# The first attention with its weights computed a second time, keys on the partitions, instead of being transposed

## The chip, the cores and the metric

The kernel runs on one core of one Trainium2 chip. The metric is the device time of one execution in microseconds (us), as the median of the runs shown. TensorE multiplies matrices, VectorE (DVE in the rows) and ScalarE (ACT) read and write PSUM and SBUF, GpSimd (POOL) works on SBUF only, and SyncE (SP) issues the DMAs.

## The reference, cut to what matters

```python
# B, N, D = 8, 512, 128; all float32
# 1: layer norm with shift and scale from c @ wmod, then causal attention with 16 heads of dimension 8
q = x @ Wq.T ;  k, v = split(x @ Wkv.T)
sim = einsum('bhid,bhjd->bhij', q * 8 ** -0.5, k);  sim = where(causal_mask, -max_float, sim)
m = max(sim, axis=-1);  e = exp(sim - m)
out = einsum('bhij,bhjd->bhid', e, v) / (sum(e, axis=-1) + 1e-8)
x = x + gate * (out @ Wo.T)
# 2: a second modulated norm, then six layers of (local attention with rotary tables, norm, gated feed-forward)
```

The change touches the attention of part 1 alone.

## The kernel before, in words

`adaln_block` runs three blocks one behind the other: `modulated_attention` (the first attention and the norms around it), `local_stack` (the six layers) and `last_residual`. Everything of the first two is kept with the dimensions on the partitions and the tokens along the free axis.

In `modulated_attention` each engine runs its own program, `batch(b)`, for b = -1 to 8, where b = 1 to 6 are turns of a hardware loop. A batch has 16 steps s, one for each head. What a step does for head s and for heads some steps back is written out in each engine's `batch`; `head_of(s, back)` names the head. Semaphores alone tie the engines together, and each engine takes its instructions in the written order. At the edges (`alive`) work of batches that don't exist is left out.

A head of 512 queries is done as four row tiles of 128 queries. Row tile i sees the keys 0 to (i + 1) * 128, so the tiles are 128, 256, 384 and 512 columns wide, 1280 together.

1. Projections. Four heads make a group. For each group, the jobs `q` and `k` (L1101) give a 128-row product whose 128 rows are four copies of the group's 32 dimensions. ScalarE rounds it (`high`, L1161 to L1165) and VectorE subtracts that from the full value in some of the copies (L1294, L1301), so that one product of two rounded operands sums high and low parts. For each head, VectorE writes `qm`, the group's q with the rows of the other three heads set to zero (`pick_head`, L1337).
2. Scores. `score` (L1056) is one matmul of rounded float32 for a row tile, into that tile's own bank; it waits until the exponential of the same tile of the head before is done.
3. VectorE adds the causal mask to the diagonal block (`mask`, L1343) and takes the negated row maximum (`maximum`, L1347).
4. ScalarE takes the exponential with the maximum as bias and the row sum as a second output (L1191, which issues an ACTIVATE and an ACTIVATION_READ_ACCUMULATOR).
5. VectorE takes the reciprocal of the four row sums (`reciprocals`, L1355, L1357), GpSimd multiplies the four row tiles by it (L1426).
6. Three steps behind, TensorE transposes the ten 128x128 blocks of the head (L1069) in two parts, ScalarE copies them out of PSUM (L1201).
7. `round` (L1095): for the four heads of a group, the weights by the values, each head in 32 columns of the array, so that four matmuls run side by side; VectorE copies the result to `aT` (L1314). `wo` (L1110) is the output projection, L1307 the gated residual.

The products other than scores and transposes (`q`, `k`, `v`, `round`, `wo`, the transposes of x, the means and variances of the norms) share one bank, `ps_m`, in the order of a hand-written list `M_JOBS` of (step, part, kind, batch offset, group). Part 0 stands inside the step, part 1 at its end. Each waits until the one before has been taken from the bank.

The norms end with one Newton step for the reciprocal root on VectorE (`finish_norm`, L1264 to L1284). GpSimd also prepares the six layers' weights and tables in the loop turns (`split`, L1408 and L1410; `rotary_tables`, L1399), and SP loads and stores them around `load(b)` and `store(b)`.

Of the kernel before, what the change touches and what calls it, by code (L numbers as in the profile page):

```python
# [7 lines left out]
ALU = mybir.AluOpType  # L8
# [5 lines left out]
P = 128  # L14
# [12 lines left out]

HID = int(DIM * 4 * 2 / 3)
# [6 lines left out]
LN_EPS = 1e-5  # L35

# [11 lines left out]
C_HEAD = C_ROT + TILES * 2 * 2 * DH  # L48
C_LOW = C_HEAD + 4
# [3 lines left out]
C_END = C_ONE + 1  # L53


def shape_constants():
# [23 lines left out]
    c[:, C_ROT:C_HEAD] = tables.reshape(TILES, P, 2 * 2 * DH).transpose(1, 0, 2).reshape(P, -1)  # L80
# [3 lines left out]

    row = np.arange(P)
    c[:, C_HEAD:C_LOW] = row[:, None] % 32 // 8 == np.arange(4)[None, :]
    c[:, C_LOW] = -1.0 * (row // 64 == 1)
    c[:, C_LOW + 1] = -1.0 * (row // 32 % 2 == 1)
# [3 lines left out]
def constant_views(consts):  # L92
# [9 lines left out]
        "head": consts[:, C_HEAD:C_LOW],  # L102
# [4 lines left out]
        "one": consts[:, C_ONE:C_END],  # L107
# [734 lines left out]
AH = 16  # L842
AD = DIM // AH
ATT_EPS = 1e-8

GROUP = 4
GROUPS = AH // GROUP
GP = P // GROUP
SCORE_BANKS = 4

ROW_AT = [i * (i + 1) // 2 * P for i in range(TILES)]
ROWS_END = TILES * (TILES + 1) // 2 * P

KEY_AT = {0: 0, 1: 512, 3: 896, 2: 1024}
PROB_BUFS, PROBT_BUFS = 4, 8

SPLIT_STEPS = (2, 9, 13)
TABLE_STEPS = (0, 4, 6, 11)


def modulated_attention(nc, w, const_sb, mod, xT, x_done, x1_dram, w_split, tables):

    ident, ones_mean, causal, head, low_q, low_k, one = (
        const_sb[k] for k in ("ident", "ones_mean", "causal", "head", "low_q", "low_k", "one"))
# [14 lines left out]
    with ExitStack() as ctx:  # L890
# [6 lines left out]
        def bank(name, n=1):  # L897
# [5 lines left out]
        wmod = sb("wmod", [P, 6 * DIM])  # L903
        wqk = sb("wqk", [P, 2, GROUPS, P])
# [8 lines left out]
        q_full = sb("q_full", [P, N])  # L913
        high = sb("high", [P, N], F32R)
        q4, k4 = sb("q4", [P, 2, N], F32R), sb("k4", [P, 2, N], F32R)
        qm = sb("qm", [P, 2, N], F32R)
        v_pad = sb("v_pad", [P, TILES, AH, GP])
        probs = sb("probs", [P, PROB_BUFS, ROWS_END])
        probT = sb("probT", [P, PROBT_BUFS, ROWS_END])
        nmx = sb("nmx", [P, 2, TILES])  # L920
        den = sb("den", [P, 2, TILES])
        rden = sb("rden", [P, 2, 2, TILES])
        aT = sb("aT", [P, GROUPS, N])
        qk_scale = sb("qk_scale", [P, 2, DEPTH, 2 * DH])
# [4 lines left out]
        ps_score = [bank(f"score{i}") for i in range(SCORE_BANKS)]  # L929
        ps_t = bank("t", 3)  # L930
        ps_m = bank("m")
# [7 lines left out]
        zeroed = sem("zeroed")  # L939
# [5 lines left out]
        rden_own, weights_ready = (  # L945
            sem(k) for k in ("rden_own", "weights_ready"))

        t_ready, t_copied = [sem("t_ready_0"), sem("t_ready_1")], [sem("t_copied_0"), sem("t_copied_1")]

# [593 lines left out]
```

## Time and profile before

| | us |
|---|---|
| median of 3 runs | 4414.89 (4414.82 to 4419.62) |
| the profiled execution | 4412.12, with a span of 4410.3 |
| first attention and its norms | from 0 to 877.6 of the span |
| local stack | from there to about 4390 |

The profile is of one execution. Its page gives the busy time of each engine over the whole span; the views used below are a table of windows, which cuts the span into stages, the waits, the groups of instructions by line and shape, and stretches of the timeline. A row of the timeline merges instructions of one line that run on: its second number runs from the first one's start to the last one's end, and the mark "x4" says how many. The clock column is the share of TensorE's full clock that was granted.

### The profile page before, as it was taken

The numbers are of one execution on the slowest core, as the hardware profiler recorded it, in microseconds if no ns is written. First come the engines' busy times: TensorE is split into PE (matmuls) and PEld (weight loads), VectorE is DVE, ScalarE is ACT, GpSimd is POOL, SyncE is SP. The second block draws the span as 40 slices with busy tenths as digits, with TensorE's granted clock in tenths as the row PEclk, the third lists the DMA queues.
The fourth block names the chain that finished last, engine by engine and source line by source line (L and its number), as shares of the span: only waits on it lengthen the run. The fifth ranks groups of instructions, "written<-read, shape, count | busy, mean of one in ns | idle before, by whom it ended". The sixth has DMA issues, their size and how long they took to land. (4 is left out here: it accounts for less than half of the span.)

```text
span 4410.3 us, 109941 instructions
## 1 busy us (share of the span) xinstructions
PE 3768.9 (85%) x41516; PEld 2856.2 (65%) x41516; DVE 3571.7 (81%) x5298; ACT 2656.4 (60%) x4035; POOL 2895.4 (66%) x2520
## 2 busy tenths in 40 slices
PE   5666666669999899998999989999899999899996
PEld 3444444357777777776777767777677777677774
DVE  6777777678888788887888878888888888888884
ACT  5666666546666566656566656656566656566663
POOL 3555555357777677676767666777677676667672
PEclk9888888889999999999999999999999999999998
DMA  1111111032222322223222232222322222222221
GB/s 38 53 53 53 53 53 45 8 90 64 55 60 56 92 59 62 56 58 91 62 55 62 56 88 65 55 58 54 89 60 67 56 56 78 70 60 63 56 55 58
DMA packets 157205, 267.21 MB, mean 61 GB/s; under 512 B 32062, under 2 KB 51644, under 8 KB 152380
## 3 DMA queue, kind: packets, MB, share of 16 engines
q1 hardware_dynamic: 157116, 266.19, 22.1%
q8 instruction: 36, 0.59, 0.1%
q14 instruction: 53, 0.43, 0.0%
HBM read 44.81 MB, written 26.21 MB: 16 GB/s over the span
## 5 line engine op out<-in xcount | busy, mean ns | idle before, releaser
L789 POOL TENSOR_TENSOR st_qk_rot<-st_qk_rot,st_qk_sq 128x1024 f32<-128x1024 f32 x384 | 920.4, 2397 | 939.6 <-DVE st_qk_sq L686 939.6
L429 PE MATMUL st_ps<-st_wqkv,st_xs 128*128 128x512 f32 x3456 | 956.7, 412 | 66.2 <-DMA st_wqkv<-wqkv_parts 37.7
L537 ACT ACTIVATE st_qk_sq<-st_ps 128x1024 f32<-128x1024 f32 x384 | 393.9, 1026 | 652.6 <-PE st_ps L429 652.0
L429 PEld LDWEIGHTS st_ps<-st_wqkv,st_xs 128*128 128x128 f32 x3456 | 612.4, 190 | 231.4 <-issue 97.8
L809 POOL TENSOR_TENSOR st_qk_rot<-st_qk_rot,st_rn 128x1024 f32<-128x1024 f32 x384 | 722.7, 1903 | 15.0
L1426 POOL TENSOR_TENSOR at_probs<-at_probs,at_rden 128x128 f32<-128x128 f32 (+3 forms) x512 | 361.8, 738 | 389.6 <-DVE at_rden L1357 389.6
L668 DVE TENSOR_REDUCE st_nt<-st_qk_sq 128x16 f32<-128x1024 f32 x384 | 465.7, 1213 | 175.5 <-ACT st_qk_sq L537 175.4
L686 DVE TENSOR_TENSOR st_qk_sq<-st_ps,st_rot 128x512 f32<-128x512 f32 x768 | 490.2, 678 | 0.0
L672 DVE TENSOR_TENSOR st_qk_rot<-st_ps,st_rot 128x1024 f32<-128x1024 f32 x384 | 465.9, 1213 | 8.6 <-PE st_ps L444 8.6
L444 PE MATMUL st_ps<-consts_sb,st_qk_rot 128*128 128x128 f32 x3072 | 403.0, 274 | 27.9 <-DVE st_hid L769 16.5
L437 PEld LDWEIGHTS st_ps<-st_oT,st_wo 128*128 128x128 f32 x3072 | 368.8, 192 | 79.4 <-issue 75.8
L1191 ACT ACTIVATE at_probs<-at_score,at_nmx 128x128 f32<-128x128 f32 (+3 forms) x512 | 269.1, 527 | 249.0 <-DVE at_nmx L1347 244.3
L444 PEld LDWEIGHTS st_ps<-consts_sb,st_qk_rot 128*128 128x128 f32 x3072 | 357.1, 141 | 93.7 <-DVE st_hid L769 36.3
L568 ACT ACTIVATE st_k_bd<-st_ps 64x1024 f32<-64x1024 f32 x384 | 389.4, 1014 | 3.7 <-PE st_ps L444 1.4
L437 PE MATMUL st_ps<-st_oT,st_wo 128*128 128x128 f32 x3072 | 379.2, 277 | 1.4 <-ACT st_probT L598 1.2
L457 PE MATMUL st_ps<-st_k_bd,st_qT 128*32 128x128 f32 x12288 | 376.1, 275 | 1.8 <-ACT st_v_tok L582 1.8
L1056 PE MATMUL at_score<-at_k,at_qm 128*128 128x128 f32 (+3 forms) x512 | 239.9, 510 | 159.8 <-ACT at_probs L1191 117.6
L469 PE MATMUL st_ps<-st_v_bd,st_probT 128*32 128x128 f32 x12288 | 375.2, 274 | 0.0
L837 POOL TENSOR_TENSOR st_s<-st_s,st_mx 128x1024 f32<-128x1024 f32 x192 | 365.8, 1905 | 9.9 <-DVE st_mx L711 9.9
L707 DVE TENSOR_TENSOR st_s<-st_ps,consts_sb 128x1024 f32<-128x1024 f32 x192 | 234.5, 1221 | 146.4 <-PE st_ps L457 146.4
L457 PEld LDWEIGHTS st_ps<-st_k_bd,st_qT 128*32 128x32 f32 x12288 | 324.4, 110 | 34.4 <-ACT st_v_tok L582 26.2
L469 PEld LDWEIGHTS st_ps<-st_v_bd,st_probT 128*32 128x32 f32 x12288 | 323.8, 110 | 23.0
(125 smaller groups left out, 6828.4 us busy)
## 6 DMA issues: line engine op xcount, KB each, us to landing
st_v_bd<-st_v_tok SPq DMA_DIRECT2D x1152, 128.0 KB, 2.3
st_v_bd<-st_v_tok SPq DMA_DIRECT2D x672, 64.0 KB, 2.1
wqkv_parts<-at_w_parts SPq DMA_DIRECT2D x18, 1024.0 KB, 4.5
st_wqkv<-wqkv_parts SPq DMA_DIRECT2D x18, 1024.0 KB, 5.7
at_w_raw<-in_wqkv SPq DMA_DIRECT2D x18, 512.0 KB, 4.1
rotary_tables<-at_rot SPq DMA_DIRECT2D x6, 512.0 KB, 2.8
st_rot<-rotary_tables SPq DMA_DIRECT2D x24, 128.0 KB, 2.4
st_wo<-in_wo SPq DMA_DIRECT2D x6, 512.0 KB, 4.2
```

The costliest lines, as they stand in the source:

```text
L429: last = pe.matmul(out[:, c * 512:(c + 1) * 512], xs[:, x_part, t * P:(t + 1) * P], rhs, start=(n == 0), stop=(n == len(PASSES) - 1))
L437: last = pe.matmul(out[:, 0:P], wo[:, c, :], oT[:, c * P:(c + 1) * P], start=(c == 0), stop=(c == IC - 1))
L444: last = pe.transpose(out[:, c * P:(c + 1) * P], src[:, c * P:(c + 1) * P], ident)
L457: last = pe.matmul(out[g * WIN:(g + 1) * WIN, c * P:(c + 1) * P], qT[:, par, c * P + g * WIN:c * P + (g + 1) * WIN], k_bd[:, c, :, key:key ...
L469: last = pe.matmul(out[g * WIN:(g + 1) * WIN, c * P:(c + 1) * P], probT[:, c * P + g * WIN:c * P + (g + 1) * WIN], v_bd[:, par, g, :, c * ...
L537: act.activation(qk_sq[:, cols_of(a)], slot_of("qk"[a], 0, t), ACT.Square).then_inc(squared[a], 1)
L568: last = act.activation(k_bd[rows, :, a, WIN + t1 * P:WIN + (t1 + 1) * P], src[rows, :, :], ACT.Copy)
L668: dve.tensor_reduce(nt[:, 2 + par, heads], qk_sq[:, cols].rearrange("p (h d) -> p h d", d=DH), AX.X, ALU.add).then_inc(ss_sum, 1)
L672: dve.tensor_tensor(qk_rot[:, cols].rearrange("p (h d) -> p h d", d=DH), slot_of("qk"[a], 0, t).rearrange("p (h d) -> p h d", d=DH), rot[: ...
L686: last = dve.tensor_tensor(dst[:, :, g, :], src[:, :, 1 - g, :], sines.unsqueeze(1).to_broadcast([P, HEADS, DH // 2]), ALU.mult)
L789: pool.tensor_tensor(qk_rot[:, cols], qk_rot[:, cols], qk_sq[:, cols], ALU.add).then_inc(rot_done[a], 1)
L809: pool.tensor_tensor(view, view, rn[:, par, heads_of(a)].unsqueeze(2).to_broadcast([P, HEADS, DH]), ALU.mult).then_inc(normed[a], 1)
```

## The change

- The scores are computed twice. The first time as before, by rows, for the maximum alone. The second time with keys on the partitions and queries on the columns (`scores_by_key`), six steps behind (`LAG`). The second product holds the weights already in the layout in which `round` wants them, so ScalarE's exponential writes `probT` directly, and the transposes, their copies, `probs`, and GpSimd's multiplication go.
- The rows of a group are laid out anew: head c has rows 32c to 32c + 31, 8 of them spare. A score matmul uses the 32 rows of its head alone, so `qm` goes. The negated maximum of each query is put into two of the spare rows of q as a high and a low part, where k has ones: the second product comes out with the maximum subtracted. `max_parts`, `max_rest`, the transposes `mt` and one addition on VectorE per group do that. The low-by-low product is not formed, and the factor 8 ** -0.5 moves into the exponential.
- The causal mask is added on TensorE, as a product of the identity and the mask that accumulates onto the scores, in both products.
- The row sum is a column of ones beside v: it comes out of `round` in row 8 of each head's 32. The jobs `den` (4 matmuls with 4 columns), a reciprocal and a copy on VectorE, `rd` (4 transposes) and a multiplication of `aT` do the division per group, after `round`. ScalarE takes `round` out of the bank.
- Three units a head instead of four row tiles: (512), (384 and 128), (256), each in one bank. The other jobs get two banks in turn, with a new list. The Newton step of the norms goes to GpSimd; `split` and `rotary_tables` stand at other steps, and SP stores x1 after the second split and the tables.

```diff
+    part, of_max = row % 32 // 8, row % 32 < 2
+    c[:, C_LOW] = -1.0 * (part == 3)
+    c[:, C_LOW + 1] = -1.0 * (part == 2) + of_max
+ROW_UNITS = (((3, 0),), ((2, 0), (0, 3 * P)), ((1, 0),))
+KEY_UNITS = ((0,), (1, 3), (2,))
-SPLIT_STEPS = (2, 9, 13)
-TABLE_STEPS = (0, 4, 6, 11)
+SPLIT_STEPS = (2, 6, 14)
+TABLE_STEPS = (0, 3, 5, 7)
-        M_JOBS = [(0, 0, "round", -1, 2), (1, 0, "q", 0, 1), (2, 0, "k", 0, 1), (3, 0, "x", 1, 0),
...
+        M_JOBS = [(0, 0, "den", -1, 1), (0, 1, "mt", -1, 3), (1, 0, "q", 0, 1), (1, 1, "rd", -1, 1), (2, 0, "k", 0, 1),
+                  (3, 0, "round", -1, 2), (3, 1, "x", 1, 0), (4, 0, "den", -1, 2), (4, 1, "mt", 0, 0),
+                  (5, 0, "q", 0, 2), (5, 1, "rd", -1, 2), (6, 0, "k", 0, 2), (6, 1, "mean0", 1, 0),
+                  (7, 0, "round", -1, 3), (8, 0, "den", -1, 3), (8, 1, "mt", 0, 1), (9, 0, "rd", -1, 3),
+                  (9, 0, "q", 0, 3), (9, 1, "v", 0, 0), (10, 0, "var0", 1, 0), (10, 0, "k", 0, 3),
+                  (10, 1, "wo", -1, 0), (11, 0, "round", 0, 0), (11, 1, "mean1", -1, 0), (12, 0, "den", 0, 0),
+                  (12, 1, "mt", 0, 2), (12, 1, "var1", -1, 0), (13, 0, "q", 1, 0), (13, 1, "rd", 0, 0),
+                  (14, 0, "k", 1, 0), (15, 0, "round", 0, 1)]
@@ SP, one turn of the loop @@
                     split_weights(b - 2, 0)
-                    store(b - 2)
                     split_weights(b - 2, 1)
                     store_tables(b - 2)
+                    store(b - 2)
                     split_weights(b - 2, 2)
@@ TensorE @@
-                    pe.matmul(ps_score[i][:, 0:(i + 1) * P], qm[:, h % 2, i * P:(i + 1) * P],
-                              k4[:, h // GROUP % 2, 0:(i + 1) * P], start=True, stop=True).then_inc(scores_ready, 1)
+                def scores(b, h, u):
+                        pe.wait_ge(max_ready, count(b, 0, AH * UNITS, (h - 1) * UNITS + u))
+                    for n, (i, at) in enumerate(ROW_UNITS[u]):
+                        pe.matmul(ps_s[u][:, at:at + (i + 1) * P], q4[strip(c), g, i * P:(i + 1) * P],
+                                  k4[strip(c), g, 0:(i + 1) * P], start=(n == 0), stop=False)
+                def mask(u):
+                    for n, (i, at) in enumerate(ROW_UNITS[u]):
+                        last = pe.matmul(ps_s[u][:, at + i * P:at + (i + 1) * P], ident_r[:, :], causal_r[:, :],
+                                         start=False, stop=(n == len(ROW_UNITS[u]) - 1))
+                    last.then_inc(scores_ready, 1)
+                def scores_by_key(b, d, h, u):
+                        pe.wait_ge(exp_ready, count(b, d, AH * UNITS, (h - 1) * UNITS + u))
+                    for n, j in enumerate(KEY_UNITS[u]):
+                        pe.matmul(ps_t[:, KEY_AT[j]:KEY_AT[j] + N - j * P], k4[strip(c), g, j * P:(j + 1) * P],
+                                  q4[strip(c), g, j * P:N], start=(n == 0), stop=False)
+                def mask_by_key(u):
+                    for n, j in enumerate(KEY_UNITS[u]):
+                        last = pe.matmul(ps_t[:, KEY_AT[j]:KEY_AT[j] + P], causal_r[:, :], ident_r[:, :],
+                                         start=False, stop=(n == len(KEY_UNITS[u]) - 1))
+                    last.then_inc(t_ready, 1)
+                        dt, ht = head_of(s, LAG)
+                        for u in range(UNITS):
+                            if alive(b, 0):
+                                scores(b, s, u)
+                            if alive(b, dt):
+                                scores_by_key(b, dt, ht, u)
+                            if alive(b, 0):
+                                mask(u)
+                            if alive(b, dt):
+                                mask_by_key(u)
+                            if u == 1:
+                                m_products(b, s, 0)
                         m_products(b, s, 1)
@@ ScalarE @@
+                    act.activation(probT[:, h % PROBT_BUFS, UNIT_COLS[u]], ps_t[:, UNIT_COLS[u]], ACT.Exp,
+                                   scale=float(AD) ** -0.5).then_inc(exp_ready, 1)
+                        act.activation(aT[:, g, :], src[:, :], ACT.Identity, bias=eps_den).then_inc(taken["round"], 1)
@@ VectorE, one step @@
+                        for u in range(UNITS):
+                                maximum(b, s, u)
+                            took = {0: jobs_at(s - 1, 0, "q", "k") +
+                                    jobs_at(s - 1, 1, "mt", "rd", "x", "wo", "mean0", "mean1", "var0", "var1"),
+                                    1: (), 2: jobs_at(s, 0, "den", "rd", "var0")}[u]
+                        if s == 11 and alive(b, 1):
+                            gain(b, 1, False)
+                        if s == 12 and alive(b, 1):
+                            finish_norm(b, 1, False)
+                        if s == 13 and alive(b, -1):
+                            gain(b, -1, True)
+                        if s == 15 and alive(b, -1):
+                            finish_norm(b, -1, True)
@@ VectorE, before the first batch @@
+                dve.memset(wqk[:, :, :, :], 0.0).then_inc(spread, 1)
+                for r in range(1, GROUP):
+                    dve.tensor_copy(wqk[:, :, :, :].rearrange("p a g (h r d) -> p (a g) h r d", h=GROUP, r=GROUP)[:, :, :, r, :],
+                                    by_head).then_inc(spread, 1)
@@ GpSimd @@
+                def newton_step(b, d, second):
+                    pool.tensor_tensor(square, root_, root_, ALU.mult).then_inc(newton[second], 1)
+                    pool.tensor_tensor(square, square, variance, ALU.mult).then_inc(newton[second], 1)
+                    pool.tensor_tensor(square, three[:, 0:1].to_broadcast([P, N]), square, ALU.subtract).then_inc(newton[second], 1)
+                    pool.tensor_tensor(centred, centred, square, ALU.mult).then_inc(normed[second], 1)
-                            last = pool.tensor_tensor(row, row, rden[:, h % 2, 1, i:i + 1].to_broadcast([P, (i + 1) * P]),
-                                                      ALU.mult)
```

The order of a unit on TensorE is: rows of head s, keys of head s - 6, mask of the rows, mask of the keys.

## Rows read from the trace of the kernel before

**Rows 1.** Page, busy time of each engine, its share of the span.
```profile
PE 3768.9 (85%) x41516; PEld 2856.2 (65%) x41516; DVE 3571.7 (81%) x5298; ACT 2656.4 (60%) x4035; POOL 2895.4 (66%) x2520
```

**Rows 2.** Windows by stage: us; busy PE, PEld, DVE, ACT, POOL; clock, DMA share, GB/s.
```profile
0.00:37.70 37.70, 12.05 (x24) 5.36 (x24) 12.16 (x28) 5.20 (x8) 0.21 (x4) 1.00 0.27 89
37.70:119.50 81.80, 60.46 (x328) 39.42 (x328) 67.49 (x200) 61.86 (x172) 44.06 (x64) 0.90 0.03 11
119.50:764.50 645.00, 431.52 (x2381) 270.17 (x2377) 476.85 (x1248) 396.58 (x1074) 373.57 (x469) 0.85 0.15 53
764.50:850.80 86.30, 62.61 (x358) 39.06 (x358) 64.55 (x189) 61.70 (x172) 42.20 (x61) 0.89 0.01 4
850.80:877.60 26.80, 15.30 (x102) 6.94 (x94) 7.90 (x14) 5.78 (x9) 2.75 (x4) 0.82 0.03 10
...
897.00:4390.00 3493.00, 3178.00 (x38304) 2489.55 (x38304) 2916.01 (x3599) 2118.50 (x2590) 2432.60 (x1920) 0.99 0.24 63
```

**Rows 3.** One source line (residual of attention): durations, first and last start.
```profile
L1307 DVEq FUSED_REGOPS  x6: 105/105/110, 155.4 to 693.2; - x6
```

**Rows 4.** Waits in 100 to 800 us: total us, times, longest.
```profile
POOL at_probs L1426 <- DVE at_rden L1357: 294.7, 96, 8.1
ACT at_probs L1191 <- DVE at_nmx L1347: 222.6, 175, 6.7
...
DVE at_score L1343 <- PE at_score L1056: 135.0, 99, 6.2
PE at_score L1056 <- ACT at_probs L1191: 106.0, 79, 6.7
```

**Rows 5.** Groups by line and shape, 100 to 800 us: busy us, mean ns.
```profile
L1069 PE MATMUL at_t<-consts_sb,at_probs 128*128 128x128 f32 x1056 | 176.4, 305 | 10.7 <-ACT at_probT L1201 9.9 <-POOL at_probs L1426 0.6
...
L1343 DVE TENSOR_TENSOR at_score<-at_score,consts_sb 128x128 f32<-128x128 f32 x422 | 123.8, 293 | 135.0 <-PE at_score L1056 135.0
L1426 POOL TENSOR_TENSOR at_probs<-at_probs,at_rden 128x512 f32<-128x512 f32 x106 | 116.9, 1103 | 0.0
...
L1201 ACT ACTIVATE at_probT<-at_t 128x768 f32<-128x768 f32 x106 | 85.5, 807 | 0.0
L1191 ACT ACTIVATION_READ_ACCUMULATOR at_probs<-at_score,at_nmx 128x1 f32 x422 | 83.8, 199 | 0.0
...
L1191 ACT ACTIVATE at_probs<-at_score,at_nmx 128x512 f32<-128x512 f32 x106 | 73.2, 691 | 19.0 <-DVE at_nmx L1347 16.8
L1347 DVE TENSOR_REDUCE at_nmx<-at_score 128x1 f32<-128x512 f32 x105 | 71.5, 681 | 0.0
...
L1337 DVE TENSOR_SCALAR at_qm<-at_q,consts_sb 128x512 fp32r<-128x512 f32 x106 | 58.2, 549 | 13.9 <-issue 11.0 <-DVE xT_sb L1280 1.9 <-DVE at_hT L1284 0.6
...
L1355 DVE TENSOR_SCALAR at_rden<-at_den 128x4 f32<-128x4 f32 x106 | 36.5, 344 | 25.7 <-ACT at_probs L1191 20.8 <-issue 1.5
...
L1347 DVE TENSOR_REDUCE at_nmx<-at_score 128x1 f32<-128x128 f32 x106 | 29.6, 279 | 0.0
```

**Rows 6.** Whole program, groups of GpSimd by line and shape.
```profile
L816 POOL TENSOR_TENSOR st_xc<-st_rstd 128x512 f32<-128x512 f32 x48 | 70.7, 1473 | 22.2 <-ACT st_rstd L614 22.2
```

**Rows 7.** Timeline of TensorE in the local stack, 1003.5 to 1007 us.
```profile
1004.08 1.67 PE L429 MATMUL st_ps<-st_wqkv,st_xs 128*128 128x512 f32 x6
```

**Rows 8.** Timeline of TensorE, 400.5 to 404.2 us.
```profile
400.54 0.63 PE L1069 MATMUL at_t<-consts_sb,at_probs 128*128 128x128 f32 x4 [0.20 <-ACT at_probT L1201]
401.10 2.36 PE L1095 MATMUL at_m<-at_probT,at_v_pad 128*32 128x512 f32 x32
403.39 0.44 PE L1056 MATMUL at_score<-at_k,at_qm 128*128 128x384 f32 x1
```

**Rows 9.** Timeline of the attention's end, 850 to 878 us.
```profile
850.03 3.60 PE L1095 MATMUL at_m<-at_probT,at_v_pad 128*32 128x512 f32 x32
...
862.23 3.67 PE L1110 MATMUL at_m<-at_aT,at_wo 128*128 128x512 f32 x8 [0.90 <-DVE at_aT L1314]
...
876.63 0.98 DVE L1280 TENSOR_SCALAR xT_sb<-at_xc,mod_sb 64x512 f32<-64x512 f32 x2
```

More of the change, by code:

```diff
@@ L927, in modulated_attention @@
         w_parts = sb("w_parts", [P, 2, INNER], F32R)
-        ps_score = [bank(f"score{i}") for i in range(SCORE_BANKS)]
-        ps_t = bank("t", 3)
-        ps_m = bank("m")
+        ps_s = [bank(f"s{i}") for i in range(UNITS)]
+        ps_t = bank("t", UNITS)
+        ps_m = [bank("m0"), bank("m1")]
         w_in, x_in, x1_out, scale_in = sem("w_in"), sem("x_in"), sem("x1_out"), sem("scale_in")
@@ L1121, in m_product @@
                         pe.wait_ge(squared[second], count(b, d, 1, 0))
-                        last = pe.matmul(ps_m[:, :], ones_mean, sq[:, second, :], start=True, stop=True)
+                        last = pe.matmul(out[:, :], ones_mean, sq[:, second, :], start=True, stop=True)
                     last.then_inc(ready[kind], 1)
@@ L1203, in batch @@
                 def batch(b):
                     for s in range(AH):
[L1205 to L1213 removed]
+                        dt, ht = head_of(s, LAG)
@@ new lines, in batch @@
+                        for u in range(UNITS):
+                            if alive(b, dt):
+                                exponentials(b, dt, ht, u)
+                            if u == 0:
+                                d, h = head_of(s, 1)
+                                if h % GROUP == GROUP - 1 and alive(b, d):
+                                    max_parts(b, d, h // GROUP)
+                            took = {0: jobs_at(s - 1, 1, "v"), 1: jobs_at(s - 1, 0, "var0") + jobs_at(s - 1, 1, "mean0", "mean1", "var1"),
+                                    2: jobs_at(s, 0, "round", "q", "k")}[u]
@@ L1289, in take @@
                 def take(b, job):
                     kind, d, g = job
[L1291 to L1302 removed]
+                    src = m_bank(kind, g)
@@ L1350, in reciprocals @@
[L1350 to L1357 removed]
+                        dve.tensor_scalar(var[:, kind == "var1", :], src[:, :], LN_EPS, None, ALU.add).then_inc(taken[kind], 1)
@@ new lines, in maximum @@
+                def maximum(b, h, u):
+                    g, c = divmod(h, GROUP)
+                    dve.wait_ge(scores_ready, count(b, 0, AH * UNITS, h * UNITS + u))
+                    if u == 0 and c == 0 and not (isinstance(b, int) and b == 0 and g < 2):
+                        dve.wait_ge(max_split, count(b, 0, GROUPS, g - 2))
+                    for i, at in ROW_UNITS[u]:
+                        last = dve.tensor_reduce(nmx[:, g % 2, i, c:c + 1], ps_s[u][:, at:at + (i + 1) * P],
+                                                 AX.X, ALU.max, negate=True)
+                    last.then_inc(max_ready, 1)
```

355 lines of the change are left out of this document (174 added, 181 removed), and 4 rows, old and new, of the table M_JOBS.

## The prediction

> **What bounds the kernel now.** The page [rows 1] shows TensorE busy 85% of the span and VectorE 81%, but these are means over stages, so I went to the windows by stage. The change touches 877.6 us [rows 2]: 37.7 ahead of the first scores, 81.8 for batch 0, 645.0 for the six turns of the loop, 86.3 for batch 7 and 26.8 behind it. A turn is 107.5 us; one line that runs once a turn confirms it, (693.2 - 155.4) / 5 = 107.6 [rows 3]. So a step of one head takes 6.7 us. In the loop no engine is full: TensorE 67%, VectorE 74%, ScalarE 61%, GpSimd 58%, and the granted clock is 0.85, against 0.99 in the local stack.
>
> The waits say why [rows 4]. A score tile waits for the exponential of the head before (106 us), the exponential for the maximum (223), VectorE's mask for the scores (135), GpSimd for the reciprocals (295). That is one ring, scores, mask, maximum, exponential, scores, and TensorE's queue is in order: a product of the single bank `ps_m`, or a transpose that waits for GpSimd or a copy, holds up the next score and with it the ring. The bound is this ring plus what stands in it, not the sum of any one engine. The local stack (3493 us, TensorE at 91%) is untouched, and the blocks follow one another, so what the attention gains the kernel gains.
>
> **What goes.** From the groups [rows 5], per head. VectorE: four masks 4 x 0.29, `qm` 0.55, reciprocals 0.34 and about 0.18: 2.2 us. ScalarE: four accumulator reads 4 x 0.20 and two copies 0.81 and some 0.6, and four exponentials become three (0.69 twice and about 0.45): 4.3 becomes 1.8. GpSimd: 1.10 for the widest tile, about 2.8 in all, which is 269 of its 374 us in the loop [rows 2], so 17 a turn are left. TensorE: ten transposes.
>
> **The ring after.** The maximum alone now frees a bank of row scores, and the exponential only that of key scores. Each is needed a whole step later. So neither is a term as long as a step is longer than VectorE's or ScalarE's own work: VectorE has 1.93 a step for maxima (0.68 and 0.28 are its ends [rows 5]) and some 33 operations of 0.7 a turn, 54 us; ScalarE 30 + 19 x 0.63 = 42; GpSimd 17 + 8 Newton operations of at most 1.47 [rows 6] = 29. What is left to set the step is TensorE, whose work I sum at full clock.
>
> **TensorE's sum, per step.**
> - Rounded matmuls of 512 columns: six in 1.67, one lasts about 0.4, so starts are (1.67 - 0.4) / 5 = 0.25 apart [rows 7]. The 1280 columns of a head cost 0.64 for rows and 0.64 for keys.
> - If the two run side by side, being in different 32-row strips, the pair costs 0.25 + 0.45 + 0.13 = 0.83 in place of 1.28. For it: `round` has 32 matmuls in four column strips, and takes 2.36 [rows 8], not four times that. No row shows row strips. I take 1.05.
> - Eight mask products of 128 columns. Transposes of that width start (0.63 - 0.305) / 3 = 0.11 apart [rows 5, 8]: 8 x 0.11 = 0.88. 0.11 is with their weight loads.
> - Changes between strips and full array: two per unit, six per head. The last transpose starts at 400.54 + 0.63 - 0.305 = 400.87, `round` at 401.10 [rows 8]: 0.23 in place of 0.11, so 0.12 for the change, and up to 0.11 more for a load that can't run ahead. Bounds 0.10 and 0.25; I take 0.17, so 1.0 a step.
> - Other products per turn: a float32 product is two passes, and eight passes take 3.67 [rows 9], 0.46 each. `q` and `k` 16 passes 7.4, `wo` 3.7, means and variances 3.7, `round` 4 x 2.36 = 9.4, `v` and `x` 1.3: 25.5. New: `mt` and `rd` 32 x 0.11 = 3.5, `den` 32 passes with a full load each, 3.5. With 31 first loads of 0.11: 35.9, 2.2 a step.
>
> Together 1.05 + 0.88 + 1.0 + 2.2 = 5.1 a step, 82 a turn. Three jobs wait for VectorE within their step: `v` at step 9 behind `rd`, `wo` at 10 behind `var0`, `var1` at 12 behind `den`: the last maximum 0.4 and a taking of 0.7, 1.1 each. Behind them in TensorE's queue stand the next scores, so they are lost: 3.3. A turn is **85 us**. The other jobs alternate between two banks and find theirs taken a step before; that is the cover, and without it each would cost the same 1.1.
>
> One rule bears on the changes of mode. The Trainium skill (TensorEngine Tiling, Key Properties) says that changing the tiling mode drains TensorE. The trace agrees, with 0.23 in place of 0.11 [rows 8]. A reader who priced the matmuls alone would have 4.1 a step, a turn of 69.
>
> **The moves.** The norms' Newton step goes to GpSimd, 4 x 1.3 in place of some 3 us on VectorE; in the loop it has the time from step 11 to the end of 12, some 8 us, and its own queue is empty there (split at 6 and 14). If it is late, `finish_norm` holds VectorE and then `q` at step 13. SP stores x1 at step 11 now; behind it stand the last third's load (needed at 14, three steps) and the load of x (needed at step 3 of the next turn). I cost both at nothing; a late one would stop GpSimd, or TensorE at `x`, for the excess.
>
> **The sum.** Six turns: 6 x (85 - 107.5) = -135. Batch 0: six steps without the second product at about 2.8 and ten at 4.7 are 64, -18. Batch 7 lacks the next batch's jobs (4): 81, -5. Ahead of the first scores VectorE fills and spreads `wqk` and clears more, and the Newton step is in the open: +4. Behind the last: six heads instead of three are still to come, at some 2.2 us, and `den`, `rd` and the Newton step are exposed before the last write (876.63 [rows 9]): +10. In all -144. The profiled execution, 4412.1, becomes 4268; it stands 2.8 below the median, so **4270**.
>
> **Bounds.** Low: strips side by side (0.83), changes at 0.10, no late bank: 16 x (0.83 + 0.88 + 0.6 + 2.1) = 71, 14 less a turn, with the static batches 4175. High: 1.28, changes at 0.25, first loads in full: 16 x 5.9 = 94 and 4 for waits, 13 more a turn: 4370.
>
> **Rivals.**
> - Slower, by the clock. TensorE may be granted 1.2 GHz while it works in strips of 32 rows. `round` takes 3.60 where it takes 2.36 [rows 8, 9] when the clock falls within it. At half clock throughout, a turn is 82 x 2 = 164, six of them +339, with batches 0 and 7 at the same rate (+116) and the edges about 4880. It decides when 82 / clock passes 104, at a mean clock under 0.79. For it: the stage has 0.85 now, though that is with TensorE idle a third of the time. Against it: the local stack, dense, has 0.99 [rows 2]. At an unchanged 0.85 a turn is 100 and the time 4365.
> - The ring stays. A wait of one engine takes the place of the old ones: the taking of a job, `max_rest` behind `max_parts`, or VectorE's order (maxima behind `q`, `k`, `wo`), so that TensorE idles as often. A turn of 95 to 100: 4335 to 4365. For it: all five queues are in order, and 31 jobs instead of 19 are handed over. Against it: two banks, and a step of slack.
> - Cheaper than summed. Both scores side by side and changes at 0.10: 4175 to 4215. The Trainium skill (TensorE: Matmul & The Clock Gate, Part 3) says that matmuls in different row groups run concurrently; no row here shows it.
> - No change: the removed work was all beside the ring, turn near 107. Against it: masks and exponentials are in the ring. 4400 to 4420.
>
> **Chances and range.** Forecast, with its own range of 4215 to 4335: 0.65. Cheaper 0.12, the ring stays or the clock stays at 0.85 0.13, no change 0.02, half clock 0.08. The range 4175 to 4370 holds the first three but for their ends, 0.86. A time within 0.2%, 9 us, is what this measurement can't tell from none: faster 0.89, same 0.03, slower 0.08.
>
> **What would show it.** Right: in the loop TensorE over 90% busy at a clock above 0.95, a turn of 80 to 90, the maximum waiting for TensorE and no longer TensorE for ScalarE, GpSimd under 40%. The 128-column mask groups 0.11 apart, and about 0.2 between a mask and the next strip. Wrong: row and key matmuls starting together (the sum is too high), a clock near 0.5 (too low), TensorE idle at `wo`, `v` or `var1` by more than 1 us each, VectorE waiting for GpSimd before `hT`, or a tail beyond 37 us.

## The result: 7.5% slower, and where the time went

| | us |
|---|---|
| after, median of 4 runs | 4746.84 (4731.79 to 4757.48) |
| before, median of 4 runs | 4414.85 (4405.14 to 4419.62) |
| after / before | 1.0752, 95% interval 1.0713 to 1.0792 |
| profiled execution after | 4738.39, with a span of 4736.6 |

The forecast was 4270 with a range of 4175 to 4370. The sign was wrong.

The page of the kernel after, busy time of each engine, the granted clock in 40 slices, and the queue that brings the engines their instructions:

```profile
PE 4172.2 (88%) x42284; PEld 3085.0 (65%) x42284; DVE 3365.0 (71%) x4472; ACT 2415.3 (51%) x3173; POOL 2609.1 (55%) x2072
...
PEclk9666665689999999999999999999999999999998
...
q8 instruction: 389, 6.37, 0.6%
```

TensorE has fewer idle gaps than before and more busy time [rows 1]. Two things stand out: the clock of the first fifth of the program, and 389 packets of instructions where the page of before has this row:

```profile
q8 instruction: 36, 0.59, 0.1%
```

The windows by stage after, with the cuts put where the stages now end (the columns are those of [rows 2]):

```profile
37.70:215.30 177.60, 170.68 (x662) 99.10 (x662) 76.84 (x158) 47.96 (x96) 16.63 (x16) 0.79 0.06 23
215.30:781.80 566.50, 546.56 (x2462) 315.86 (x2460) 258.46 (x521) 179.66 (x356) 130.83 (x110) 0.63 0.15 51
781.80:973.00 191.20, 175.46 (x808) 100.67 (x806) 73.44 (x149) 58.23 (x115) 23.96 (x18) 0.64 0.04 13
973.00:992.00 19.00, 0.00 (x0) 0.00 (x0) 14.47 (x5) 2.00 (x3) 0.00 (x0) 0.50 0.72 250
992.00:4720.00 3728.00, 3260.57 (x38304) 2558.82 (x38304) 2920.21 (x3601) 2118.58 (x2590) 2432.36 (x1920) 0.96 0.24 61
```

The line that runs once a turn, the gated residual [rows 3], after:

```profile
L1387 DVEq FUSED_REGOPS  x6: 99/99/110, 215.3 to 781.8; - x6
```

So a turn takes (781.8 - 215.3) / 5 = 113.3 us, in place of 107.6. The attention ends at 973.0, in place of 877.6: 95 us more. The local stack, whose code the change does not touch, takes 3728 us where it took 3493 [rows 2], with the same 38304 matmuls. The two spans are 326 us apart, so with 95 before that point, 231 come behind it. So there are two causes to find, one in the attention and one in code that was not changed.

The waits of the loop, 200 to 800 us (total, times, longest), against [rows 4]:

```profile
POOL at_sq L1480 <- ACT at_rstd L1243: 473.2, 12, 86.8
ACT at_probT L1250 <- PE at_t L1093: 411.8, 241, 7.5
DVE at_nmx L1412 <- PE at_s L1074: 327.5, 182, 7.5
...
POOL at_w_parts L1470 <- DMA at_w_raw<-in_wqkv: 53.9, 10, 6.6
...
PE at_m L1150 <- DVE at_var L1403: 5.7, 6, 1.0
PE at_m L1126 <- DVE at_mx_cols L1420: 5.4, 5, 2.9
...
PE at_m L1144 <- DVE at_aT L1382: 4.5, 5, 0.9
PE at_m L1166 <- DVE at_rden_rows L1376: 3.1, 6, 0.6
```

The ring is gone, as forecast: everybody waits for TensorE, and TensorE hardly for anybody. It is 96% busy in the loop (546.56 / 566.5), at a mean clock of 0.63, so most of the time at 1.2 and not 2.4 GHz.

One step of a head after, on TensorE, at half clock:

```profile
399.75 0.79 PE L1068 MATMUL at_s<-at_k,at_q 32*128 32x512 f32 x1
399.75 0.79 PE L1087 MATMUL at_t<-at_q,at_k 32*128 32x512 f32 x1
400.47 0.47 PE L1074 MATMUL at_s<-at_causal_r,at_ident_r 128*128 128x128 f32 x1
400.74 0.41 PE L1093 MATMUL at_t<-at_ident_r,at_causal_r 128*128 128x128 f32 x1
401.08 0.68 PE L1068 MATMUL at_s<-at_k,at_q 32*128 32x384 f32 x1
401.09 0.68 PE L1087 MATMUL at_t<-at_q,at_k 32*128 32x384 f32 x1
```

The row and the key scores start together, so the row strips do run side by side. The Trainium skill (TensorE: Matmul & The Clock Gate, Part 3) says they would, and the trace agrees, with starts at most 0.01 us apart. The first unit takes 401.08 - 399.75 = 1.33 us. The same unit in a stretch whose granted clock is 1.00 (the run e1_after_pad below, one that keeps this code):

```profile
331.65 0.38 PE L1071 MATMUL at_s<-at_k,at_q 32*128 32x256 f32 x1
...
331.97 0.33 PE L1077 MATMUL at_s<-at_causal_r,at_ident_r 128*128 128x128 f32 x1
332.13 0.27 PE L1096 MATMUL at_t<-at_ident_r,at_causal_r 128*128 128x128 f32 x1
...
337.04 0.50 PE L1071 MATMUL at_s<-at_k,at_q 32*128 32x512 f32 x1
337.05 0.49 PE L1090 MATMUL at_t<-at_q,at_k 32*128 32x512 f32 x1
337.47 0.33 PE L1077 MATMUL at_s<-at_causal_r,at_ident_r 128*128 128x128 f32 x1
337.64 0.28 PE L1096 MATMUL at_t<-at_ident_r,at_causal_r 128*128 128x128 f32 x1
337.84 0.44 PE L1071 MATMUL at_s<-at_k,at_q 32*128 32x384 f32 x1
...
338.28 0.44 PE L1077 MATMUL at_s<-at_causal_r,at_ident_r 128*128 128x128 f32 x2
338.56 0.38 PE L1096 MATMUL at_t<-at_ident_r,at_causal_r 128*128 128x128 f32 x2
```

There it takes 337.84 - 337.04 = 0.80.

### The profile page after: what moved, and what is told of

It is laid out like the page before. It is cut to its first block and busy times, and to the rows that moved or that the text cites. A ratio compares the mean times of both kernels' runs of the same rounds, so it can differ in the third digit from the quotient of the medians.

```text
span 4736.6 us, 108599 instructions
## 1 busy us (share of the span) xinstructions
PE 4172.2 (88%) x42284; PEld 3085.0 (65%) x42284; DVE 3365.0 (71%) x4472; ACT 2415.3 (51%) x3173; POOL 2609.1 (55%) x2072
## 5 line engine op out<-in xcount | busy, mean ns | idle before, releaser
L441 PE MATMUL st_ps<-st_wqkv,st_xs 128*128 128x512 f32 x3456 | 1015.3, 432 | 239.0 <-issue 171.7
L441 PEld LDWEIGHTS st_ps<-st_wqkv,st_xs 128*128 128x128 f32 x3456 | 650.8, 202 | 416.8 <-issue 271.4
L1412 DVE TENSOR_REDUCE at_nmx<-at_s 128x1 f32<-128x512 f32 (+3 forms) x512 | 238.3, 487 | 479.0 <-PE at_s L1074 477.7
L1250 ACT ACTIVATE at_probT<-at_t 128x512 f32<-128x512 f32 (+1 forms) x384 | 201.9, 526 | 594.1 <-PE at_t L1093 594.0
L456 PE MATMUL st_ps<-consts_sb,st_qk_rot 128*128 128x128 f32 x3072 | 429.6, 286 | 28.1 <-DVE st_hid L781 16.7
L456 PEld LDWEIGHTS st_ps<-consts_sb,st_qk_rot 128*128 128x128 f32 x3072 | 382.5, 148 | 100.6 <-DVE st_hid L781 36.4
L1480 POOL TENSOR_TENSOR at_sq<-at_rstd 128x512 f32<-128x512 f32 x16 | 17.1, 1068 | 730.2 <-ACT at_rstd L1243 730.2
```

The costliest lines, as they stand in the source:

```text
L441: last = pe.matmul(out[:, c * 512:(c + 1) * 512], xs[:, x_part, t * P:(t + 1) * P], rhs, start=(n == 0), stop=(n == len(PASSES) - 1))
L456: last = pe.transpose(out[:, c * P:(c + 1) * P], src[:, c * P:(c + 1) * P], ident)
```

## The experiments

Twelve kernels ran, each once, but for f1_picked, which ran four times; the kernel before gave 4405.38 to 4420.81 us in seven runs beside them, so the differences that matter below are well clear of the noise. The numbers of the local stack come first, those of the attention after it. A "turn" is of the attention's loop, "clock" the mean granted clock over it, "stack turn" the time of one layer and batch in the local stack, as the median distance between the starts of a line that runs once in each (70.95 before, 76.97 after). "Packets" are those of the instruction queue, q8 on the page.

### Why the untouched local stack became slower

The first theory: nothing in the data or the DMAs of the stack has changed, but TensorE's program ahead of it has another length, so the same loop body lies elsewhere against the blocks in which instructions are fetched. The test moves the body by instructions that do nothing.

```diff
 # e1_after_pad: kernel after;  e2_before_pad: kernel before;  TensorE's program of the attention
+                for _ in range(128):
+                    pe.sem_inc(pad, 1)
```

> The changed kernel with 128 empty semaphore increments at the very start of TensorE's program, where TensorE waits for the weights anyway. Two stages became slower: the attention (877.6 to 973 us) and the local stack, whose code is the same (a turn of its loop 71.0 to 76.9 us). In the local stack of the changed kernel a queue of kind instruction moves about nine packets of 16 KB a turn, and before it moved none. Theory A, where the code lies: TensorE's loop body of 1657 instructions is 6.5 such packets long; started at another place in a packet it touches one packet fewer and stays on the core. Then 128 instructions more ahead of it bring the turn back to 71.0, the instruction packets in the loop go, the local stack loses some 230 us, and the whole is near 4510, with the attention at 973 as before. Theory B, the attention leaves something behind (memory addresses, clock, data): the turn stays at 76 to 77 and the whole near 4740.

> The kernel before with the same 128 increments at the same place. Theory A: its loop body now starts in the half of a packet where it touches one more; the turn goes from 71.0 to about 77 us, instruction packets run all through the local stack, and the whole becomes about 4645 with the attention unchanged at 878. Theory B: no change, 4412 to 4420.

Measured: e1_after_pad took 4503.56 us, and its stack turn is 70.98 at a clock of 0.99, all as expected. e2_before_pad took 4749.14, with a stack turn of 79.11 at 0.95: slower, as expected, but by 337 us where I had written 233. The rows of instruction packets of the two pages, e1_after_pad first:

```profile
q8 instruction: 38, 0.62, 0.1%
```

```profile
q8 instruction: 432, 7.08, 0.6%
```

The attention changed little (turns of 111.0 where after has 113.3, and 108.0 where before has 107.6; the 2 us of the first are not explained). So 128 empty instructions take 235 us off the kernel after and put 337 us on the kernel before. The data, the DMAs and the instructions of the stack are the same with and without them, so theory B is out. The next run asked whether a shift of 32 instructions is enough, one more than the 31 between before and after, with the increments in the pause before the stack, where they hide behind VectorE's clearing of buffers:

```diff
 # f4_before_32: kernel before; TensorE's program of the local stack, ahead of its first wait
+                for _ in range(32):
+                    pe.sem_inc(pad, 1)
                 pe.wait_ge(zeroed, 2)
```

> The kernel before with 32 empty increments on TensorE between the attention and the local stack, where TensorE is idle for 17 us. Theory A in its sharp form: the loop body is 1657 instructions, 256 fill a packet, and it stays on the core while it touches 7 packets, so its start may lie at 0 to 135 in a packet. The kernel before fits and the changed one, 31 further, doesn't, so 32 further than before doesn't either: a turn of 79, instruction packets all through the stack, and 4730 to 4745. Rival: it takes a larger shift, as the 128 of e2_before_pad; then 4412.

Measured: 4650.29 us, stack turn 76.89, 387 packets of instructions. The direction was right and the size was not, 237 us where I had written about 325: I had taken e2_before_pad's turn for the price of not fitting, but the price depends on the place. The loop body is 1657 TensorE instructions in the compiled program, 6.5 blocks of 256. Its start, counted in instructions modulo 256 (up to a constant, since what the launch puts ahead isn't counted), against what the runs showed:

| kernel | start mod 256 | packets | stack turn |
|---|---|---|---|
| e3_full_rows, e4_no_mask, e1_after_pad | 228 | 38 in e1_after_pad | 70.96 to 70.98 |
| f1_picked | 250 | 39 | 70.96 |
| before | 69 | 36 | 70.95 |
| after | 100 | 389 | 76.97 |
| f4_before_32 | 101 | 387 | 76.89 |
| e2_before_pad | 197 | 432 | 79.11 |

All rows agree with one reading: the body touches either seven blocks or eight, and with eight it is fetched anew in every turn. (1657 instructions touch seven blocks where the start lies 0 to 135 behind a block's edge. With the edge anywhere from 198 to 220 in this count, 228, 250 and 69 do, and 100, 101 and 197 don't.) The packets come all through the stack: from 1500 to 1750 us 20 of them start in after and 29 in e2_before_pad, none in before or e1_after_pad. Over 48 turns (38304 matmuls, 798 a turn) that is (389 - 36) / 48 = 7.4 packets a turn for after and (432 - 36) / 48 = 8.3 for e2_before_pad. After and f4_before_32 have the same place in the block but for one instruction, and agree to 0.1 us a turn though they are different kernels. The Trainium skill (Runtime: NRT & Kernel Launch, Instruction fetch mechanics) gives TensorE 2048 instructions in blocks of 256 and says that a taken branch to a block outside the current window of two forces a fetch. The rows of after, f4_before_32 and e2_before_pad show such fetches. Those of before and e1_after_pad differ from the page: a loop of 6.5 blocks branches back 47 times there, and the queue moves 36 and 38 packets in the whole program. That the limit is seven blocks is inferred from the six rows; it was not measured by itself.

All kernels below carry 75 or 128 increments, but for f2_before_strips, whose program has before's length. So their stacks are as before (stack turns of 70.95 to 70.98) and only the attention differs.

### Why the attention became slower

Theory: TensorE's work is about what I summed, and the low clock comes from the strips of 32 rows. Rival: the work itself is longer than summed. Two runs change what the array does and keep all the rest.

```diff
 # e3_full_rows
-  q4[strip(c), g, ...], k4[strip(c), g, ...]
+  q4[:, g, ...], k4[:, g, ...]        (both products)
 # e4_no_mask: strips as in the kernel after, mask(u) and mask_by_key(u) left out
```

> The changed kernel (with the 128 increments) where both score products use all 128 rows of a group in place of the 32 of the head: the result is the sum over four heads' scores, which is not the reference's attention. Columns, masks and everything else stay. Theory S, the strips of 32 rows cost TensorE its clock: the granted clock of the attention's loop goes from 0.63 to above 0.9; rows and keys no longer run side by side, which costs 0.4 us a step at full clock; the changes of mode go. A turn of 113 becomes 75 to 85 and the attention ends near 730 to 780. Theory M, the narrow mask products or sheer density do it: the clock stays at 0.6 to 0.7, and a turn becomes 120 to 130, since the side-by-side saving is lost.

> The changed kernel (with the 128 increments) without the mask products on TensorE, so the attention is not causal within the diagonal blocks. The strips stay. Per head 8 products of 128 columns and the six changes of mode are gone, 1.9 us at full clock by the prediction's prices. Theory S: the clock stays at or under 0.65 in steps without other products, and the turn falls only by the removed work at half clock, 16 x 2.5 to 3.5, to 60 to 75. Theory M: the clock rises over 0.9, and the turn falls to 50 to 55, where VectorE and ScalarE set it.

e3_full_rows took 4210.81 us: a turn of 77.4 at a clock of 0.99, in the range of theory S, and its attention ends at 681, earlier than I had given. e4_no_mask took 4301.39: a turn of 89.5 at 0.68. Its clock stayed low as theory S has it, but its turn missed the 60 to 75 by far: without the masks TensorE is busy only 82% of the loop, and the removed work gave back 21.5 us a turn, not 40 to 56. The windows of their loops, five turns each, e3_full_rows first:

```profile
154.00:541.00 387.00, 348.85 (x2463) 265.45 (x2462) 262.92 (x520) 178.64 (x355) 132.45 (x110) 0.99 0.21 75
```

```profile
190.00:637.00 447.00, 365.84 (x1821) 181.30 (x1819) 249.38 (x520) 169.73 (x355) 131.26 (x111) 0.68 0.18 65
```

The kernel with four times the rows per score product is 34 us a turn quicker than the one with strips, with the same number of matmuls. The one with a quarter of the matmuls left out keeps its low clock. So the strips cost clock; masks, and the six changes of mode a step that they bring, are not needed for that. And the strips save nothing at full clock: the first unit of a step with all rows, where the clock is 1.00,

```profile
301.87 0.44 PE L1071 MATMUL at_s<-at_k,at_q 128*128 128x512 f32 x1
302.15 0.39 PE L1090 MATMUL at_t<-at_q,at_k 128*128 128x512 f32 x1
302.38 0.22 PE L1077 MATMUL at_s<-at_causal_r,at_ident_r 128*128 128x128 f32 x1
302.44 0.27 PE L1096 MATMUL at_t<-at_ident_r,at_causal_r 128*128 128x128 f32 x1
302.55 0.45 PE L1071 MATMUL at_s<-at_k,at_q 128*128 128x384 f32 x2
```

takes 0.68 us, against 0.80 in strips: the second product comes 0.28 behind the first, but a mask follows 0.23 behind it and the next unit 0.11 behind the last mask, where strips have 0.42 and 0.20.

Then strips were put into the kernel before, and into one product only of the kernel after:

```diff
 # f2_before_strips: kernel before, qm[:, ...], k4[:, ...] -> qm[0:GP, ...], k4[0:GP, ...] in the score product
 # f3_keys_full: kernel after, keys with q4[:, ...], k4[:, ...], rows still in strips
```

> The kernel before, with its score product over the first 32 rows of the group alone (one part of the four that the sum needs, so not the reference's scores); nothing else is changed, its ten transposes per head are full. Theory S, matmuls in strips of 32 rows cost TensorE its clock in any kernel: the granted clock of the loop falls from 0.85 to 0.65 to 0.75, and a turn rises from 107.6 to 112 to 118. Rival: the clock needs the double product in strips or its density; then 0.82 to 0.87 and 107 to 110.

> The changed kernel with the key product alone over all 128 rows (the sum of four heads' scores, not the reference's), the row product in strips. A dose between e1_after_pad (clock 0.65, turn 111) and e3_full_rows (0.99, 77). Theory S in proportion: the clock between 0.75 and 0.9 and a turn of 88 to 98. Rival, the changes of mode (as many as in e1, and now between rows and keys too) cost as much as the clock: a turn over 100 at a clock over 0.85.

f2_before_strips: turn 114.0 at a clock of 0.78, where before has 107.6 at 0.85; 4479.72 us. The kernel before, too, loses clock and time with strips, with one score product at a time and TensorE 77% busy; the turn is as expected, the clock a little above the 0.65 to 0.75 that I had given. f3_keys_full: turn 120.2 at 0.69, 4555.07 us. I had expected a clock between the two kernels and a turn of 88 to 98; it came out slower than either. The key scores no longer start beside the row scores but behind them (400.89 and 401.20 in its timeline), so the work grew, and the clock hardly rose. "The clock goes by the rows in use" was therefore not enough, and the last four runs separate rows from changes of mode (a change is a product of one tile size behind one of another).

```diff
 # g1_half_rows:      both products over the 64 rows of half(c) = slice(c // 2 * 64, (c // 2 + 1) * 64)
 # g2_full_no_mask:   all 128 rows, masks left out
 # h1_half_no_mask:   64 rows, masks left out
 # h2_full_half_mask: all 128 rows, masks with ident_r[0:64, :], causal_r[0:64, :]
```

> The kernel after, but each score product takes the 64 rows of two heads instead of the 32 rows of one, in both products (so it sums the scores of two heads; not the reference's), and 128 empty semaphore increments stand in front of TensorE's program of the local stack, which keep that loop where its instructions are not fetched again (about 4 us). Row scores of head s and key scores of head s - 6 still lie in different halves, so they can still run side by side; masks, jobs and the number of changes of mode are those of the kernel after. Theory 'the clock falls with the share of the array's rows that the scores use': a clock between the 0.65 of strips of 32 and the 0.99 of all 128 rows, 0.75 to 0.9, and a turn of 80 to 97 us; time 4240 to 4380. Rival 'the clock falls because two tiles run at once or because the mode changes': clock 0.60 to 0.70 and a turn of 108 to 114 as with strips, time 4490 to 4510. Rival 'any half is as good as the whole': clock above 0.95, turn 68 to 76, time 4150 to 4210.

> The kernel after with scores over all 128 rows (sum of four heads) and without the mask products (both leave the reference's computation), and the same 128 increments ahead of the local stack. Against the run with full rows and masks (turn 77.4 us at a clock of 0.99) it prices the eight mask products per step at full clock without any change of mode. Theory 'TensorE is the bound there and a mask is a 128-column start': 16 x 8 x 0.11 = 14 us less a turn, 61 to 66 us, unless VectorE's or ScalarE's own work (54 and 42 us by my sum) takes over; time 4110 to 4150. Rival 'masks fill gaps that the waits leave': turn 70 to 77, time 4170 to 4210, with TensorE under 85% busy. The clock is expected above 0.95; should it fall well below, TensorE's idle time and not only the rows in use would count.

> The kernel after with score products over the 64 rows of two heads and without the mask products (both leave the reference's computation), 128 empty increments ahead of the local stack as in the other runs. Row and key scores still lie in different halves and can run side by side, so together they use all 128 rows, and the changes of mode fall from six a step to those around the other jobs. Known: 64 rows with masks had a clock of 0.74, 32 rows without masks 0.68, 128 rows without masks 0.98. Theory 'the changes of mode cost the clock, once most rows are in use': clock above 0.92, turn 60 to 72 us, time 4090 to 4180. Theory 'the rows of the single product count, whatever runs beside it': clock 0.70 to 0.85 and a turn of 75 to 88, time 4200 to 4290.

> The kernel after with score products over all 128 rows (sum of four heads) and mask products over 64 rows only (half of the mask is left out), 128 empty increments ahead of the local stack. There are as many changes of mode as in the kernel after, six a step, but the long products use all rows. Theory 'the changes of mode cost the clock': clock 0.60 to 0.75, turn 105 to 115 us, time 4440 to 4500. Theory 'the rows that the long products use set the clock': clock above 0.90; each change then adds about 0.1 us to the turn of 77.4 us measured with full rows and full masks, 16 x 6 x 0.09 = 9, so 80 to 90 us; time 4220 to 4290.

| rows of a score product | masks | turn | clock | whole, us |
|---|---|---|---|---|
| 32 (e1_after_pad) | 128 rows | 111.0 | 0.65 | 4503.56 |
| 32 (e4_no_mask) | none | 89.5 | 0.68 | 4301.39 |
| 64 (g1_half_rows) | 128 rows | 101.0 | 0.74 | 4411.48 |
| 64 (h1_half_no_mask) | none | 73.7 | 0.89 | 4198.38 |
| 128 (h2_full_half_mask) | 64 rows | 99.0 | 0.84 | 4402.32 |
| 128 (e3_full_rows) | 128 rows | 77.4 | 0.99 | 4210.81 |
| 128 (g2_full_no_mask) | none | 68.3 | 0.98 | 4141.60 |

The loops of h1_half_no_mask and of g1_half_rows, and h2_full_half_mask's in stretches, where the clock differs from one to the next though the code repeats:

```profile
157.00:522.00 365.00, 287.33 (x1806) 150.93 (x1806) 243.00 (x519) 167.96 (x353) 131.90 (x110) 0.89 0.22 79
```

```profile
201.00:706.00 505.00, 480.87 (x2461) 281.25 (x2460) 260.63 (x520) 179.51 (x355) 131.00 (x110) 0.74 0.16 57
```

```profile
200.00:300.00 100.00, 96.23 (x530) 63.82 (x532) 53.83 (x109) 38.48 (x75) 26.13 (x22) 0.88 0.17 59
300.00:400.00 100.00, 96.67 (x543) 64.21 (x536) 55.37 (x115) 39.32 (x78) 31.08 (x26) 0.91 0.19 65
400.00:500.00 100.00, 96.94 (x430) 63.90 (x432) 46.16 (x91) 31.65 (x62) 21.36 (x18) 0.73 0.14 50
```

Neither rival of the last two runs came out alone: both land between. Fewer rows cost clock with no masks at all (0.98, 0.89, 0.68). Changes of mode cost clock too: masks over all rows added to scores over 64, which brings the changes, take it from 0.89 to 0.74, while the same masks added to scores over 128, which brings none, leave it (0.98 and 0.99). h2_full_half_mask (0.99 to 0.84) points the same way, but its masks also use fewer rows, so alone it doesn't separate the two. g1_half_rows came out just outside what I had given, in clock, turn and time. g2_full_no_mask took the time expected, with a turn 2 us longer. It kept its clock with TensorE 83% busy over its loop, where e4_no_mask, 82% busy (365.84 of 447), didn't, so idle time is not what separates these runs. Why the chip grants the clock this way is left open.

At full clock a change costs near what the prediction had, 0.17: h2_full_half_mask's unit of 384 and 128 columns takes 304.48 - 303.17 = 1.31 us, e3_full_rows' 303.56 - 302.55 = 1.01, with two changes more: 0.15 each. (With it the expectation for h2_full_half_mask, which took 0.09, would have been some 6 us a turn higher.)

```profile
303.17 0.51 PE L1071 MATMUL at_s<-at_k,at_q 128*128 128x384 f32 x2
303.51 0.45 PE L1090 MATMUL at_t<-at_q,at_k 128*128 128x384 f32 x2
303.89 0.43 PE L1077 MATMUL at_s<-at_causal_r,at_ident_r 64*128 64x128 f32 x2
304.17 0.38 PE L1096 MATMUL at_t<-at_ident_r,at_causal_r 64*128 64x128 f32 x2
304.48 1.06 PE L1134 MATMUL at_m<-consts_sb,at_aT 128*128 128x4 f32 x8
```

### A version that beats both

Full rows keep the clock, and f1_picked computes the reference with them: the rows of the other three heads are zero in a copy of q for the one head. VectorE writes that copy for the row scores (the step that the change had removed), GpSimd, idle for three quarters of the loop, the one for the key scores, two steps ahead.

```diff
+  dve.tensor_scalar(q_row[:, h % 2, :], q4[:, g, :], head[:, c:c + 1], None, ALU.mult)
+  pool.tensor_tensor(q_key[:, h % 4, :], q4[:, g, :], head[:, c:c + 1].to_broadcast([P, N]), ALU.mult)
-  q4[strip(c), g, i * P:(i + 1) * P], k4[strip(c), g, 0:(i + 1) * P]
+  q_row[:, h % 2, i * P:(i + 1) * P], k4[:, g, 0:(i + 1) * P]
-  k4[strip(c), g, j * P:(j + 1) * P], q4[strip(c), g, j * P:N]
+  k4[:, g, j * P:(j + 1) * P], q_key[:, h % 4, j * P:N]
```

> A version that computes the reference and keeps all of the change but the strips. VectorE writes, for each head, the group's q with the other heads' rows zero (as the kernel before did) for the row scores, and GpSimd the same for the key scores, two steps ahead in four buffers; both products then use all 128 rows. 75 empty increments ahead of the local stack's TensorE program, where TensorE is idle, put its loop where it stays on the core. If the strips were the only fault of the attention: the clock is above 0.95 as in e3_full_rows, VectorE has 16 x 0.5 us more a turn and GpSimd 16 x 1.1, both beside TensorE, a turn is 77 to 81, the attention ends at 685 to 705 and the whole is 4210 to 4235, a ratio of 0.955 to 0.96. Rival: the picks come late behind GpSimd's splits and Newton steps (4.4 and 5 us), TensorE waits and the clock falls with it: a turn of 85 to 95, 4260 to 4330.

Measured: 4245.93 us (4243.69 to 4248.39, 4 runs), 0.9618 of before, 95% interval 0.9601 to 0.9635. The turn of 81.4 and the time are 0.4 and 11 us above what was expected; the clock is 0.975. Its loop in windows:

```profile
168.00:575.00 407.00, 360.58 (x2462) 268.51 (x2460) 306.31 (x601) 180.06 (x356) 220.05 (x191) 0.97 0.20 71
```

Rows that only multiply by zero are enough: the sums are those of the strips, and the clock is close to that of full rows, 0.975 and 0.987.

## Why the prediction was wrong, point by point

- **The failed step: the clock.** "TensorE, whose work I sum at full clock" was the step, and "the local stack, dense, has 0.99" what I held for it. Dense it is, 96% busy, and granted 0.63. The rival "slower, by the clock" named the cause, strips of 32 rows, and I gave it 0.08. The rival's point of decision, "a mean clock under 0.79", was too high: the kernel after is slower at 0.63, but g1_half_rows has 0.74 and a turn of 101.0, under before's 107.6. That changes of mode cost clock as well was in no rival. The row that should have weighed more was the 0.85 of the stage before beside the 0.99 of the stack [rows 2]: I put it down to TensorE's idle third, and e3_full_rows and f2_before_strips show that what runs counts as well. The rival's price, 164 a turn, was of half clock throughout and with my sum; measured 113.3.
- **A second step failed: the local stack "is untouched", "so what the attention gains the kernel gains".** No rival held that a stage with the same code could change. It cost 231 us of 326. Without it the kernel after would be at 4503.56 (e1_after_pad), still slower than before.
- **TensorE's sum** was a little high. 111.0 us at 0.650 is 72 at full clock, where I had 82 and 3.3 for waits. That scaling is rough, since not every part of a step doubles at half clock (1.33 against 0.80). Units at full clock, from the timeline of e1_after_pad, with 0.20 behind the last mask: 0.80 for 512 columns, 0.68 for 256 (331.65 to 332.13 and 0.20), 1.03 for 384 and 128 (337.84 to 338.56, a second mask of 0.11, and 0.20): 2.5 a step where I had 1.05 + 0.88 + 1.0 = 2.9. The strips side by side are most of the difference, as the rival "cheaper" said (0.22 of the 0.4, by the prediction's own two prices); changes at 0.15 were near my 0.17.
- **The rules weighed.** That a change of mode drains TensorE (the Trainium skill, TensorEngine Tiling, Key Properties): the trace agrees, with 0.15 each at full clock. Its second effect, on the clock, was in neither the rule nor my sum.
- **What goes, and the ring.** Right. VectorE's load is 258.46 / 5 = 51.7 a turn (54 summed), ScalarE's 35.9 (42), GpSimd's 26.2 (29), each from the window of five turns above.
- **The late banks.** Right in sum: 5.7, 5.4, 4.5 and 3.1 us in the waits above, 3.5 a turn where I had 3.3. One of the four is another than named: `mt`, which waits for `mx_cols`, up to 2.9.
- **The moves.** GpSimd does wait for a late load of `w_raw`, 53.9 us in ten waits, and nobody waits for GpSimd behind it: it is 23% busy. Costed at nothing, and it cost nothing.
- **Edges.** Taken together, the attention without its six turns is 973.0 - 6 x 113.3 = 293 us, against 877.6 - 6 x 107.5 = 233 before; forecast were 9 less. Batches 0 and 7 lie at the same low clock. The Newton step in the open, four GpSimd operations from 966.83 to 972.0, took 5.2.
- **No change, the ring stays.** Neither: with the clock kept, the same plan gives turns of 77 to 81 (e3_full_rows, f1_picked), and 4210.81 and 4245.93 us. So the forecast of 4270 comes within 25 us of f1_picked, but by luck: its turn of 85 was summed for strips, and that of full rows is 4 to 8 us less.

## What to carry to other kernels

Ask of a change on TensorE not only how long its matmuls are but which clock they will be granted: here tiles of 32 rows and changes between tile sizes took the clock from 0.99 to 0.65 in a stage that was 96% busy, and padding the products with zero rows took more than a quarter off the stage's turn. After any change of the instruction count, compare an untouched later loop first, its turn time and the packets of the instruction queue, before explaining the total; a loop near the size that is kept can cost more by its place than the change itself. Judge an edit to such a kernel at two placements, or pad to one that fits.

## What the runs showed of the hardware beyond that

- The clock column says 1.00 where nothing has been recorded yet. In the kernel after, the first records of the clock lie at 111 us, and the groups of 60 to 110 us, under a column of 1.00, have the durations of half clock:

```profile
L1068 PE MATMUL at_s<-at_k,at_q 32*128 32x512 f32 x8 | 6.3, 790 | 0.0
```

  790 ns, as at 399.75 above, against 500 at full clock. So the 0.79 of the window of batch 0 above is too high, and durations decide.
- An empty semaphore increment on TensorE cost 0.07 to 0.1 us at the program's start: 128 of them move the first score from 42.5 to 52.0 us in e1_after_pad and from 37.7 to 50.3 in e2_before_pad. In the pause before the stack 128 lengthen it from 19.3 to 20.3 us (g1_half_rows), and 32 or 75 leave it at 19.3 to 19.4 (f4_before_32, f1_picked).
- The price of not fitting: 353 more packets came with 231 us in after, 0.65 us each, and 396 more with 325 us of the stack in e2_before_pad, 0.8 each. The granted clock of the stack falls with the stalls, from 0.99 to 0.96 in after.
